# A product of the softplus chain moves from GpSimd to VectorE

## What is computed

```
xz = ln(h) @ in_proj_w;  xc, z = split(xz)
xc = silu(depthwise_conv3x3(xc) + conv_b)                 # 192 channels
xs = [xc by rows, xc by columns, both reversed]           # K = 4 directions
dts, Bs, Cs = split(xs @ x_proj_w)
delta = softplus(dts @ dt_w + dt_b)                       # the chain that the change touches
h_t = h_(t-1) * exp(delta_t * A) + (delta_t * u_t) * B_t  # 16 states a channel
y_t = sum over the states of h_t * C_t, + D * u_t
y = ln(sum of the four directions) * silu(z) @ out_proj_w
out = x + alpha * (h + y)
```

## Time and profile before

| | |
|---|---|
| median of 3 runs | 35,912.43 us (35,880.35 to 35,913.19) |
| the profiled execution | 35,690.79 us, its span 35,689.0 us |
| mean granted TensorE clock | 0.974 of full speed |
| PE busy | 31,817.4 us (89%) |
| DVE busy | 28,888.5 us (81%) |
| POOL busy | 27,670.9 us (78%) |
| ACT busy | 22,907.5 us (64%) |

### The profile page before, as it was taken

How to read it: one execution, slowest core, us unless ns; L and a number is a source line. 1 busy time by engine, 2 the same in 40 slices (tenths; PEclk the granted TensorE clock), 3 DMA queues, 4 the chain that set the end, 5 groups by cost and what they waited for, 6 DMA issues and landing times.

```text
span 35689.0 us, 507090 instructions
## 1 busy us (share of the span) xinstructions
PE 31817.4 (89%) x156422; PEld 8044.7 (23%) x156422; DVE 28888.5 (81%) x19623; ACT 22907.5 (64%) x36063; POOL 27670.9 (78%) x14456
## 2 busy tenths in 40 slices
PE   8998888888888888888888888888888888888888
PEld 2332222222222222222222222222222222222222
DVE  7886888888888888888888888888888888888887
ACT  4554666666666666666666666666666666666666
POOL 0001888888888888888888888888888888888888
PEclk9998999999999999999999999999999999999999
DMA  3333333333333333333333333333333333333333
GB/s 82 85 86 70 80 81 78 82 81 79 80 81 81 82 80 82 80 82 82 82 82 81 81 80 82 80 82 81 82 82 81 81 80 83 79 82 81 82 83 74
DMA packets 2982984, 2889.21 MB, mean 81 GB/s; under 512 B 2202096, under 2 KB 2202224, under 8 KB 2961200
## 3 DMA queue, kind: packets, MB, share of 16 engines
q1 hardware_dynamic: 2974144, 2808.09, 34.7%
q0 software_dynamic: 8560, 77.41, 0.6%
HBM read 1914.67 MB, written 141.30 MB: 58 GB/s over the span
## 4 chain that ended last, share of the span: by engine, by line
POOL 57%; issue 32%; POOLq 1%; PE 1%; ACT 0%; DVE 0%; SPq 0%; DMA 0%; ACTq 0%; DVEq 0%
POOL state L922 43%; POOL dd L937 4%; POOL sp_y L927 3%; POOL dd L952 2%; POOL dd L950 2%; POOL yf L966 2%; POOLq L918 0%; POOL dd L961 0%; PE dbu L1017 0%; PE yb L1032 0%; SPq L722 0%; DVE state L1429 0%; POOLq L960 0%; POOLq L920 0%; POOLq L944 0%
## 5 line engine op out<-in xcount | busy, mean ns | idle before, releaser
L922 POOL TENSOR_TENSOR state<-state,cc 128x1024 f32<-128x1024 f32 x9408 | 22377.4, 2397 | 4231.6 <-DVE state L1429 4162.4
L1429 DVE TENSOR_TENSOR_SCAN state<-state,dbu 128x1024 f32<-128x1024 f32 x9408 | 21182.7, 2274 | 4936.3 <-PE dbu L1017 3207.4
L1017 PE MATMUL dbu<-dg,du_t 64*64 64x512 f32 x75264 | 10441.5, 624 | 2802.9 <-DVE state L1429 2772.5
L1218 ACT ACTIVATE state<-dl,a_neg 128x512 f32<-128x512 f32 x18816 | 12252.6, 710 | 1068.4 <-PE yb L1032 1044.8
L1032 PE MATMUL yb<-state,mask 128*64 128x512 f32 x37632 | 11051.8, 633 | 4.5 <-POOL state L922 4.5
L1017 PEld LDWEIGHTS dbu<-dg,du_t 64*64 64x64 f32 x75264 | 2064.8, 133 | 9530.1 <-issue 9514.2
L1418 DVE TENSOR_TENSOR dg<-b_t,mask 128x1024 f32<-128x1024 f32 x3136 | 3754.9, 1197 | 400.7 <-PE dbu L1017 348.5
L1032 PEld LDWEIGHTS yb<-state,mask 128*64 128x64 f32 x37632 | 1994.6, 136 | 8284.7 <-issue 8118.6
L1285 ACT ACTIVATE sp_a<-pp 128x512 f32<-128x512 f32 x1176 | 702.4, 597 | 4822.4 <-PE pp L1098 4822.1
L225 POOL DMA_DIRECT2D act_d<-acted x32 | 16.2, 508 | 3254.2 <-DVE mixed L485 3254.2
L433 DVE SCALAR_TENSOR_TENSOR acc<-image,cw_v,acc 96x432 f32<-96x432 f32 (+2 forms) x2912 | 1687.6, 647 | 0.0
(11 more groups left out here) (166 smaller groups left out, 23855.7 us busy)
## 6 DMA issues: line engine op xcount, KB each, us to landing
cc<-cd SPq DMA_DIRECT2D x6272, 256.0 KB, 4.5
dl<-dd SPq DMA_DIRECT2D x4704, 128.0 KB, 2.3
shifted<-in_x SPq DMA_DIRECT2D x384, 392.0 KB, 12.5
xs<-xi SPq DMA_DIRECT2D x1176, 112.0 KB, 3.3
xs<-xi SPq DMA_DIRECT2D x588, 128.0 KB, 3.2
image<-in_x SPq DMA_DIRECT2D x32, 1176.0 KB, 24.5
act_d<-acted POOLq DMA_DIRECT2D x32, 1176.0 KB, 9.4
base_d<-mixed POOLq DMA_DIRECT2D x32, 1176.0 KB, 11.7
```

Source lines behind the costliest of these rows:

```text
L922: nc.gpsimd.tensor_tensor(its, its, cc[:, h, s, :], ALU.mult).then_inc(hc_done, 1)
L1017: nc.tensor.matmul(dbu[p % 2][JB * q:JB * q + JB, TOK * v:TOK * v + TOK], du_t[its, j, 128 * s + JB * h:128 * s + JB * h + JB], dg[its, h, ...
L1218: nc.scalar.activation(state[:, slot, :, m * WPX:m * WPX + WPX], dl[:, j, h, :].rearrange("p (w t) -> p w t", t=WPX), ACT.Exp, scale=a_neg ...
L1429: nc.vector.tensor_tensor_scan(its, its, dbu[p % 2][:], 0.0, ALU.mult, ALU.add).then_inc(scan_done, 1)
```

## The change

The product moves from POOL's body to DVE's, and from two steps after the chain's start to four. In DVE's order it stands after the diagonals and the work on `pp`, before `lesser` and the scan of the step. The semaphores stay the same.

```
-L_LOG, L_PROD, L_MIN, L_U = 1, 2, 5, 5
+L_LOG, L_PROD, L_MIN, L_U = 1, 4, 5, 5
...
             @block.gpsimd
-                def product(T, f, j):
-
-                    pool.wait_ge(sp_act, chain(T, f, j) + 1)
-                    nc.gpsimd.tensor_tensor(sp_y[:], sp_y[:], sp_w[:], ALU.mult).then_inc(sp_prod, 1)
...
                         if has(b):
                             times_c(b, p)
-                        for T, f, j in chains_at(b, p, L_PROD):
-                            product(T, f, j)
...
             @block.vector
+                def product(T, f, j):
+
+                    dve.wait_ge(sp_act, chain(T, f, j) + 1)
+                    nc.vector.tensor_tensor(sp_y[:], sp_y[:], sp_w[:], ALU.mult).then_inc(sp_prod, 1)
...
+                        for T, f, j in chains_at(b, p, L_PROD):
+                            product(T, f, j)
                         for T, f, j in chains_at(b, p, L_MIN):
                             lesser(T, f, j)
                         if has(b):
                             scan(b, p)
```

## The result

The changed kernel took 36,203.3 us (median of 4, 36,177.3 to 36,237.7) against 35,912.8 us of the kernel before (4 runs, 35,880.4 to 35,932.8): ratio 1.0082, 95% interval 1.0065 to 1.0100. It is slower by 290 us, where 782 us were predicted; the time lies 27 us under the range. The profiled execution took 36,221.5 us.

A forecast was written before the change was run, and what follows sets the result against it. No engine was full; DVE from scan 40 through scan 2 was taken as the path. Terms of 1.98, 1.56, 0.28 and 0.17 make 3.99 us a tile, x 196 = 782 us: 36,694 us, range 36,230 to 37,020 (own range 36,450 to 37,000).

The forecast's parts named there:

- DVE is on the path at steps 40 to 2: DVE runs without a gap from scan 40 to 47 and stays the path through scan 2.
- POOL's 1508 us buy next to nothing: Six products leave POOL, 7.7 us a tile; at step 20, on the path, 1.28 us gone buys nothing.
- a DVE operation with two SBUF operands waits for POOL's instruction: Such an operation and a POOL product exclude one another; each new product costs 0.6 to 2.93 us.
- the first rival: The DVE product waits for nothing: 1.8 us a tile, 353 us, time 36,265 us; chance 0.18.
- product at step 42: On DVE before scan 42: waits 1.38 us for POOL's step-41 product, works 0.60; +1.98 us a tile.
- product at step 1: On DVE before scan 1: finds POOL busy, waits 0.96 us, works 0.60; +1.56 us a tile.
- minimum of step 2: On DVE behind scan 1: waits 1.36 us for POOL, works 0.60; +0.28 us a tile, bounded by -1.08 and +1.25.
- step 22 and the stretch to step 25: DVE product goes first, POOL's step 21 waits; all to the step-25 transpose is 0.17 us later a tile.
- steps 8, 15, 35: Products there cost 0.1 to 0.5 us each in front of DVE gaps waiting for PE or ACT; 0 a tile.
- the last one of the sum: Profiled 35,690.8 us plus 782 gives 36,473; on the median's basis, 35,912.4 or 0.6% higher, it becomes 36,694 us.

The follow-up runs named there:

- r_psum: Changed kernel with the DVE product's second operand read from the scan's PSUM bank instead of sp_w; 36,246 us, ratio 1.0097.
- f_psum_all: Changed kernel with the product's second operand from PSUM, plus idle matmuls on PE at steps 2, 28, 36 and one at 42; 35,391 us.
- f_before_all: Kernel before, with two idle matmuls on PE at each of steps 2, 28 and 36; 35,010 us, ratio 0.9793.
- f_after_all: Changed kernel with idle matmuls on PE at steps 2, 28 and 36 and three more at step 42; 35,659 us, ratio 0.9983.
- f_four_all: Kernel before with the products of steps 8, 15, 22 and 35 on DVE, plus idle matmuls at steps 2, 28 and 36; 35,030 us.
- f_none_all: Kernel before with the softplus product left out on both engines, plus idle matmuls at steps 2, 28 and 36; 35,140 us.
- r_before: Kernel before, unchanged, run again; median 35,977 us of 12 runs, ratio 0.999.
- f_after_3: Changed kernel with idle matmuls at steps 2, 28 and 36 but none at step 42; 35,721 us.
- r_four: Kernel before with the products of steps 8, 15, 22 and 35 on DVE, the other two left on POOL; 36,171 us, ratio 1.0065.
- r_none: Kernel before with the softplus product left out on both engines; 36,283 us, ratio 1.0101.

## Why the prediction was wrong in size

The direction, the places and the mechanism were right: DVE is on the path at steps 40 to 2, POOL's 1508 us buy next to nothing (0.32 us a tile, below), and a DVE operation with two SBUF operands waits for POOL's instruction. r_psum and f_psum_all show the last for the plain product, which the trace of before could not; the first rival (no wait) fell. Its time, 36,265 us, was nearer than the forecast's 36,694, but that is luck: the product of step 42 did wait. Against the pair with an even clock, in the mean distance from the start of one scan to the next over all tiles of the two traces:

| term of the sum, us a tile | predicted | f_before_all to f_after_all |
|---|---|---|
| product at step 42 | 1.98 | 1.89 |
| product at step 1 | 1.56 | 1.42 |
| minimum of step 2 | 0.28 | 0.22 |
| step 22 and the stretch to step 25 | 0.17 | 0.10 |
| steps 8, 15, 35 | 0 | 0 |
| minimum of step 43 | 0 | -0.32 |
| sum | 3.99 | 3.31 |

The last term was not seen. At an even clock the minimum of step 43 takes 0.98 us in f_before_all and 0.95 in f_four_all, which both keep POOL's product of step 40, and 0.66 to 0.67 in f_after_all and f_none_all, which don't. In the tile that was read it took 0.67, so there was nothing to gain there; over all tiles of that trace its mean is 0.79.

The step that failed is the last one of the sum: "The median of the runs shown is 35,912.4, 0.6% above it; on that basis 36,694 us", and with it the silence of the sum before it on the clock. It takes what the profiled execution lacks to the median, 222 us, as a constant that the change leaves alone. That is the cost of a lower clock, and the change altered what the clock costs. The profile of before was of its kernel's faster kind (0.974, where most executions of r_before have 0.966); that of the changed kernel, at 0.966, lies 18 us above its median, not 222 below. Execution against execution the change cost 36,221.5 - 35,690.8 = 531 us.

So the miss of 491 us has three parts. The price at an even clock is 649 us and not 782: 133, the terms of the table. The two profiled executions differ by 531 and not 649: 119, for the clock costs the changed kernel less than it costs the kernel before. And the two medians differ by 290 and not 531: 240, because the profile of before was a favourable one. (Each part is rounded.) The last two, 359 us, are the clock's. In other words, filling PE's waits took 35,913 - 35,010 = 903 us off the kernel before and 36,203 - 35,659 = 544 us off the changed one, 359 less; this is the same sum in another order, not a second measurement.

The granted clock itself is no higher in the changed kernel: 0.966 to 0.967, where executions of the kernel before that took 35,888 to 35,931 us have 0.968 or 0.969. It is the lower clock that costs it less. In its trace 195 falls lie at step 42, where f_after_3 shows one to cost 0.3 us a tile net. That these replace dearer ones elsewhere is not shown, since no execution of the kernel before at 0.966 to 0.969 was traced. These differences are taken across chips, and the median of the kernel before moves by 300 us with the share of its kinds of executions: on the chip of f_before_all it was 35,673, and filling took 663 us off it. So the 359 hold for the medians of the first runs only, to some tens of us; the price itself, 649, is of one chip.

The rows had room for it. The earlier trace rows have no granted clock among them, though the table ahead of the prediction gives 0.974 as a mean; PE's matmuls in the window that was read were in part twice as long, behind PE's wait at step 36:

```profile
20074.11 1.53 PE L1017 MATMUL dbu<-dg,du_t 64*64 64x512 f32 x8 [1.93 <-DVE state L1429]
20075.57 1.98 PE L1032 MATMUL yb<-state,mask 128*64 128x512 f32 x4
...
20078.74 1.08 PE L1032 MATMUL yb<-state,mask 128*64 128x512 f32 x4
...
20075.00:20078.00 3.00, 3.00 (x12) 0.60 (x12) 3.00 (x3) 0.00 (x0) 2.84 (x3) 0.50 0.48 31
```

The prediction's path treated such times as durations of the work. And it lengthened PE's gap at step 42 from 1.2 to 3.1 us with no thought for what PE does behind a gap. That alone moves scan 0 by 0.9 us, which then took 0.6 to 0.7 from the product of step 1. The upper end of the prediction's own range, 37,000, doesn't follow from its reason either: 36,694 + 235 is 36,929.

What remains open: which of the kernels gets short and which gets long slow stretches behind the same 1.57 us gap. The length of the gap alone doesn't decide it: in the trace of before PE also waits 1.5 us at scan 1 and 1.7 us at scan 25 of every tile, and the clock falls behind them in one tile at most. In some kernels the falls repeat from tile to tile (in r_psum at the same three places in 192 or 193 of 196 tiles), in others not, and no run here separates the causes. Nor was it tried whether real work, moved into the gaps at steps 2, 28 and 36, would serve as well as idle matmuls.

The best kernel of all is f_before_all, the kernel before with idle matmuls in three gaps: 35,010 us, 2.1% faster than before on the same chip (0.9793, 0.9750 to 0.9837) and, across chips, 3.3% faster than the changed one.

## What to carry to other kernels

Before a trace's durations are summed against a median of runs, compare the granted clocks: the difference is a term of its own, and a change that moves waits moves it. An elementwise operation with both operands in SBUF, moved from POOL to DVE beside a busy POOL, costs the wait for POOL's instruction (1.97 instead of 0.68 us here); put it directly behind the event for which POOL waits too, or read an operand from PSUM. A gap of 1.6 to 2 us on PE can cost more than the change under study: fill such gaps first, then compare.

## What of the hardware was not expected

- The granted clock fell behind PE waits of 1.57, 1.9, 2.0 and 3.1 us, though not behind every wait of this length, and stayed at half from 20072 to 20085.5 us in r_four, while PE was never idle.
- Leaving work out made the kernel slower twice: by 310 us with the clock left alone (r_none against its kernel before, 36,283 to 35,974), and by 130 us with it evened, through the phase between DVE and POOL at the port.
- Idle matmuls of 6 x 0.78 us a tile made the kernel 663 us faster on one chip (35,673 to 35,010).
- One program has executions of two kinds on one chip, 35,590 us at a clock of 0.977 and 35,975 us at 0.966 (r_before and the runs beside it).
